# Rebuilding the tail of a fused two-layer kernel: gated cell in 128-token chunks, batches overlapped, and the experts' second layer in row tiles

## What is computed

```python
x = x + xattn(_layernorm(x), ctx)      # 16 heads of 32, softmax, Wq Wk Wv Wo
x = x + experts(_layernorm(x))         # 32 experts x 4 sets: argmax over groups of 32 tokens
x = x + gated(_layernorm(x), ctx)      # 8 heads of 64, q = norm(x), k = v = ctx
x = x + bitlinear(gelu(bitlinear(_layernorm(x), W1, b1)), W2, b2)   # 512 -> 2048 -> 512
```

```python
cs = cumsum(log_sigmoid(fg))                         # forget gates
log_D[i, j] = cs[i] - cs[j] + ig[j]   for j <= i     # else -inf
D = exp(log_D - max_j log_D)
C = (q @ k.T / 8) * D
h = C / (max(|sum_j C|, exp(-max log_D)) + 1e-6) @ v
h = h * rsqrt(mean(h * h) + 1e-6)
```

## Time and profile before

| | us |
|---|---|
| median of 3 runs | 2611.24 (2610.79 to 2611.46) |
| the profiled execution, its own time | 2620.14 |
| its span, first to last instruction | 2618.4 |
| attention, experts, tail in that span | 0 to 1107, 1113 to 1478, 1485 to 2618 |
| mean granted clock of the tensor engine, share of full | 0.902 |

### The profile page before, as it was taken

How to read it: one execution, slowest core, us unless ns; L and a number is a source line. 1 busy time by engine, 2 the same in 40 slices (tenths; PEclk the granted TensorE clock), 3 DMA queues, 4 the chain that set the end, 5 groups by cost and what they waited for, 6 DMA issues and landing times. The chain is left out here.

```text
span 2618.4 us, 43758 instructions
## 1 busy us (share of the span) xinstructions
PE 2216.2 (85%) x14571; PEld 1398.9 (53%) x14571; DVE 1524.9 (58%) x2958; ACT 1347.6 (51%) x2952; POOL 616.1 (24%) x1020
## 2 busy tenths in 40 slices
PE   7999999999999999678788449696979797979755
PEld 3666666666666666375484127353535353535432
DVE  2767676767676767423323225766666666666664
ACT  3666565656565655223324237564646454555543
POOL 1332323131323132031120012313131313131310
PEclk9999999999999999889999767797979797979777
DMA  6334343434343333166756764222122222222100
GB/s 189 95 102 137 82 137 84 138 81 139 78 142 81 109 79 103 49 176 175 239 158 201 257 237 170 97 69 81 68 81 68 81 68 81 68 81 68 37 13 17
DMA packets 193553, 289.05 MB, mean 110 GB/s; under 512 B 29440, under 2 KB 93984, under 8 KB 188128
## 3 DMA queue, kind: packets, MB, share of 16 engines
q1 hardware_dynamic: 134384, 200.32, 24.2%
q10 hardware_dynamic: 42608, 52.97, 6.4%
q0 software_dynamic: 16384, 33.59, 5.0%
HBM read 156.62 MB, written 63.05 MB: 84 GB/s over the span
## 5 line engine op out<-in xcount | busy, mean ns | idle before, releaser
L499 DVE TENSOR_REDUCE a_negmax<-a_score 128x1 f32<-128x512 f32 x512 | 346.5, 685 | 117.2 <-PE a_score L614 109.0
L434 ACT ACTIVATE a_prob<-a_score,a_negmax 128x512 f32<-128x512 f32 x512 | 354.2, 694 | 94.4 <-DVE a_negmax L499 93.5
L316 POOL DMA_DIRECT2D a_q_stack<-a_q_parts x512 | 250.8, 498 | 513.1 <-DVE a_q_parts L493 253.8
L614 PE MATMUL a_score<-a_k_stack,a_q_stack 128*128 128x512 f32 x512 | 354.6, 693 | 9.5 <-ACT a_prob L434 7.6
L622 PEld LDWEIGHTS a_turn<-a_ident,a_prob 128*128 128x128 f32 x2048 | 254.2, 141 | 134.6 <-issue 93.2
L622 PE MATMUL a_turn<-a_ident,a_prob 128*128 128x128 f32 x2048 | 309.3, 274 | 3.4 <-ACT a_perm L410 2.0
L324 DVE COPY a_probT<-a_turn 128x512 f32<-128x512 f32 x256 | 176.4, 689 | 215.8 <-PE a_turn L622 215.6
L324 ACT COPY a_probT<-a_turn 128x512 f32<-128x512 f32 x256 | 150.2, 587 | 285.3 <-PE a_turn L622 283.7
L1253 POOL TENSOR_SCALAR c_diag<-c_negm,c_aL 128x128 f32<-128x128 f32 x256 | 165.5, 664 | 362.2 <-DVEq L1474 127.5
L1711 PE MATMUL c_work<-c_xT,c_cT 64*128 64x512 f32 (+3 forms) x512 | 185.2, 510 | 39.7 <-DVE c_decay L1480 39.7
L1711 PEld LDWEIGHTS c_work<-c_xT,c_cT 64*128 64x128 f32 x512 | 105.2, 215 | 138.7 <-issue 74.4
(11 more groups left out here) (196 smaller groups left out, 3732.8 us busy)
## 6 DMA issues: line engine op xcount, KB each, us to landing
a_k_stack<-a_k_parts SPq DMA_DIRECT2D x512, 64.0 KB, 2.7
a_q_stack<-a_q_parts POOLq DMA_DIRECT2D x512, 64.0 KB, 2.3
scratch_res<-b_res SPq DMA_DIRECT2D x32, 1024.0 KB, 4.6
c_res<-scratch_res SPq DMA_DIRECT2D x32, 1024.0 KB, 9.6
b_xn<-scratch_xn SPq DMA_DIRECT2D x68, 256.0 KB, 2.7
c_hid<-in_L_ffn_W ACTq DMA_DIRECT2D x16, 1024.0 KB, 5.1
c_negm<-scratch_m SPq DMA_DIRECT2D x64, 256.0 KB, 3.4
a_xs<-in_x ACTq DMA_DIRECT2D x8, 1024.0 KB, 5.3
```

Source lines behind the costliest of these rows:

```text
L316: eng.dma_start(stack[kind][i * DH0:(i + 1) * DH0, M % 2, g, :].bitcast(F32), parts[kind][g * DH0:(g + 1) * DH0, part, :].bitcast(F32)).th ...
L434: nc.scalar.activation(prob[:, U % 4, :], score.bank(U)[:, :], ACT.Exp, bias=negmax[:, u:u + 1], accum_out=sums[:, head_of(U), tile_of(U): ...
L499: nc.vector.tensor_reduce(negmax[:, U % UNITS:U % UNITS + 1], score.bank(U)[:, :], AX.X, ALU.max, negate=True).then_inc(max_ready, 1)
L614: nc.tensor.matmul(score.bank(U)[:, :], stack["Q"][:, M % 2, g, t * P:(t + 1) * P], stack["K"][:, M % 2, g, :], start=True, stop=True).the ...
```

## The change

**Attention.** SP stores `cT` of each batch, 1 MB, to a new scratch tensor, between key stacks 2 and 3; ACT waits for that store before it writes the next batch's `cT`. The two query-stack semaphores are made in `build` and cleared at the end.

**Experts.** `inner` loses its zeros: one relu of 128 partitions per expert (4 per group instead of 16), and the second layer multiplies the 32 partitions of a set by 32 rows of `w2T`. The waits for the four result banks come first, the four matmuls follow together.

```diff
-        inner = sb("inner", [P, 2, NE, SETS, G])
+        inner = sb("inner", [P, 2, NE, G])
...
-                nc.gpsimd.memset(inner[:, :, :, :, :], 0.0).then_inc(zeroed, 1)
...
                                 for s in range(SETS):
                                     work.wait_free(pe, h * WORK + GATHERED, 4 * e + s)
-                                    nc.tensor.matmul(work.bank(s)[:, :], inner[:, (j - 1) % 2, e % NE, s, :], w2T[:, e % 2, :],
+                                for s in range(SETS):
+                                    r = slice(s * F, (s + 1) * F)
+                                    nc.tensor.matmul(work.bank(s)[:, :], inner[r, (j - 1) % 2, e % NE, :], w2T[r, e % 2, :],
                                                      start=True, stop=True).then_inc(work.full[s], 1)
...
-                                for s in range(SETS):
-                                    r = slice(s * F, (s + 1) * F)
-                                    last = nc.scalar.activation(inner[r, j % 2, e, s, :], aux.bank(j)[r, e * G:(e + 1) * G], ACT.Relu,
-                                                                bias=b1c[r, bass.ds(h * XH + (j * NE + e), 1)])
+                                last = nc.scalar.activation(inner[:, j % 2, e, :], aux.bank(j)[:, e * G:(e + 1) * G], ACT.Relu,
+                                                            bias=b1c[:, bass.ds(h * XH + (j * NE + e), 1)])
```

```diff
+    PERIOD = (("XQ", 0, -1), ("SCO", 0, 0), ("UP", 0, -1), ("W", 0, 0), ("ST", 0, 0), ("SC", 0, 1),
+              ("SCO", 1, 0), ("W", 1, 0), ("MIX", 0, 0), ("UP", 1, -1), ("W", 2, 0), ("ST", 1, 0), ("SC", 1, 1),
+              ("SCO", 2, 0), ("W", 3, 0), ("MIX", 1, 0), ("HT", 0, -1), ("DN", 0, -1), ("ST", 2, 0), ("SC", 2, 1),
+              ("SCO", 3, 0), ("W", 4, 0), ("MIX", 2, 0), ("SC", 3, 1), ("UP", 2, -1), ("W", 5, 0), ("ST", 3, 0),
+              ("HT", 1, -1), ("DN", 1, -1), ("MIX", 3, 0), ("XT", 0, 1), ("W", 6, 0), ("UP", 3, -1), ("G", 0, 1), ("W", 7, 0),
+              ("HT", 2, -1), ("DN", 2, -1), ("ROWS", 0, 1), ("HT", 3, -1), ("DN", 3, -1))
...
+                    for n in range(3):
+                        chain.step(nc.gpsimd.tensor_tensor(sq, dst, dst, ALU.mult))
+                        chain.step(nc.gpsimd.tensor_tensor(sq, sq, val, ALU.mult))
+                        chain.step(nc.gpsimd.tensor_scalar(sq, sq, -0.5, 1.5, ALU.mult, ALU.add))
+                        chain.step(nc.gpsimd.tensor_tensor(dst, dst, sq, ALU.mult))
...
+                        act.wait_ge(masked, i + 1)
+                        if i >= 4:
+                            wait_full(act, "MIX", (i - 4) // H1, (i - 4) % H1 // 2, h % 2)
+                        nc.scalar.activation(decay[:, h % 4, :], negm[:, h % 4, :], ACT.Exp).then_inc(decay_ready, 1)
...
+                    step(nc.vector.tensor_copy(st[:, 0, :], bank[:, 0:DV]))
+                    for c in range(1, LATER):
+                        last = nc.vector.scalar_tensor_tensor(st[:, c, :], st[:, c - 1, :], gbc[:, p % 2, c * P - 1:c * P],
+                                                              bank[:, c * DV:(c + 1) * DV], ALU.mult, ALU.add)
...
+                    for t in range(T):
+                        for k in range(2):
+                            last = nc.tensor.matmul(work.bank(j + k)[:, cols(t)], cT[half(k), p, cols(t)], xT[half(k), p, cols(t)],
+                                                    start=True, stop=True)
...
+                        for i in range(T):
+                            last = nc.tensor.matmul(mix.bank(j + k)[:, i * DV:(i + 1) * DV], decay[:, (2 * p + k) % 4, cols(i)],
+                                                    head_of(v, 2 * p + k)[:, i], start=i == 0, stop=i == 0, skip_group_check=True)
...
+                    for i in range(1, T):
+                        for k in range(2):
+                            last = nc.tensor.matmul(mix.bank(j + k)[:, i * DV:(i + 1) * DV], xg[half(k), p % 2, cols(i - 1)],
+                                                    state[half(k), p % 2, i - 1, :], start=False, stop=True, skip_group_check=True)
```

The last third of a period on DVE (own is batch m, old is f = m - 1, new is n = m + 1):

```diff
+                    if new:
+                        shifts(0, n)
+                    if own:
+                        states(m, 3)
+                    if old:
+                        scale_hidden(f, 2)
+                        finish(f, 1)
+                    if not old:
+                        clip_weight(6)
+                    if own:
+                        norms(m)
+                    if old:
+                        expand(f, 3)
+                        quantize_hidden(f, 2)
+                    if not old:
+                        clip_weight(7)
+                    if own:
+                        scale_heads(m)
+                    if new:
+                        rows(n)
+                    if old:
+                        scale_hidden(f, 3)
+                        finish(f, 2)
+                    if own:
+                        stats_x3(m)
+                    if new:
+                        columns(n)
+                    if own:
+                        shifts(1, m)
+                    if old:
+                        quantize_hidden(f, 3)
+                    if own:
+                        token_scales(m)
+                        quantize_tokens(m)
+                    if old:
+                        finish(f, 3)
```

1217 lines of the change are left out of this document (714 added, 503 removed).

## The result

The changed kernel takes 2648.9 us (median of 4 runs, 2648.3 to 2655.1) against 2611.4 for the kernel before in the same session: 1.0147 times as long, with 1.013 to 1.0165 as the 95% interval. The forecast was 2503. It is slower where faster was expected.

What follows compares the result with a forecast made beforehand. PE was taken to bound attention, latency of serial chains the tail. Span 2618.4 - 25 (experts) + 3 (first scores) - 61 (middle periods) - 12 (first) - 14 (last with a cell) + 1 = 2510, so 2503 us as median; range 2380 to 2605.

Steps and rivals of the forecast that it cites:

- rival 3: Tail: DVE and POOL hold each other up, +14 and +8 us, periods of 140, total 2655, slower; chance 0.11.
- The middle periods: Tail: walking DVE's order gives 118 us per period instead of 128.2, ends 104 and 130; six save 61.
- The clock: Middle period: `down` after a pause takes 5.3 us instead of 3.6, three or four bursts; +5 us per period.
- POOL's small steps: Middle period: 12 Newton steps in a chain on POOL, taken at 0.3 us each, between 0.1 and 0.6.
- First period: Tail's first period: ACT works some 62 us, then the same chain to `xq`; 92 instead of 104.5, saving 12 (0 to 25).
- Experts: Second-layer stages: fewer relus put three groups of four on the path, saving 12.5 us per stage, 25 in all.
- Until the first scores: Tail's start: one more MB at 4.4 us, fewer transposes and copies about 2 less; +3 us (0 to +10).
- Last with a cell: Tail's last period with a cell: front and scatter are missing; 100 instead of 113.6, saving 14 (0 to 30).
- Last feed-forward: End of the tail: same order, so 0, and +1 us for the second clearing of semaphores.
- row tiles: Experts' second layer: 32-row matmuls taken at the same time as 128-row ones, no gain, since PE is not waited for.
- DVE as the bound: Rival for the tail: overlap works and DVE's work bounds it, periods of 88 us, total 2290; chance 0.10.
- Experts that stay: Rival for the experts: their stages keep their length, paced by transfers, total 2528; chance 0.12.

Runs made afterwards that it cites:

- e7: e5 with POOL starting the heads' four additions only after DVE has scaled all four tiles; 2555.9 us, 0.9757 of the kernel before.
- e11: e9 with states, scatter and mix moved ahead of `down` on PE, and gelu 2 and `down` 1's copies ahead of normalizations on ACT; 2454.1 us, period 106.0.
- e12: e11 with the next batch's fourth scatter moved ahead of `down` 0 and the mix of pair 2 on PE; 2420.1 us, period 99.8.
- e10: e9 with 16, 32, 22 and 6 extra matmuls ahead of the four `down`, covering PE's waits; 2531.5 us, period 115.1.
- e9: Changed kernel with e2's and e4's orders, POOL's b2 additions behind next masks and keys, batch 0's `cT` and `v` loaded behind late `res`; 2535.5 us, period 117.6.
- e3: Changed kernel with 12 extra constant matmuls ahead of every `down`; 2636.4 us, 1.0081 of the kernel before, period 127.8.
- e4: Changed kernel with another order in the first period alone, weight pieces behind each pair's mix on PE; 2627.8 us, first period 111.8 instead of 135.4.
- e8: Kernel before with only the experts' change, second-layer matmuls reading all 128 rows instead of 32, results wrong; 2604.6 us in one run.
- e5: Changed kernel with e2's and e4's orders, batch 1's loads behind batch 0's gate rows, POOL's b2 additions behind next masks and keys; 2556.2 us, period 117.7.
- e2: Changed kernel with ACT's copies for `down` 2 ahead of the chunk weights and those for `down` 3 ahead of the tokens' rounding; 2624.7 us, period 126.1.

## Why the prediction was wrong

**The sign.** It came out on the slow side, close to rival 3's 2655, but by luck and not by rival 3's mechanism. That rival rested on one addition of the kernel before, the longest of eight:

```profile
L1532 DVE TENSOR_TENSOR c_gate_rows<-c_gate_rows x8: 678/679/1475, 1548.0 to 2435.0; 8x512 f32<-8x512 f32 x8
```

It priced DVE's lengthening at 14 us a period and POOL's at 8. In the changed kernel, what each operation of the six middle periods took beyond the shortest of its line and operands adds up to 2.8 us a period on DVE, 2.0 of them the scalings, and 4.7 on POOL. Two steps on 4 columns (L1745 and L1747, 0.97 and 1.31 us) are long in every period, while their like (L1775, L1776) take 0.15 and 0.20; an estimate from these puts 2 us more on DVE. And e7 took the contention away at its largest place and the period did not move. A number that fits is no proof of its cause.

**The middle periods, 118 forecast, 129.5 measured.** The walk on DVE named nearly all the right waits and gave them too little. From `finish` 3 on, end of each step in the period from 2088.8 us, in us:

| step | forecast | after | more than forecast since the row above |
|---|---|---|---|
| expand 0 | 9 | 7.3 | -1.7 |
| largest value 1 | 27 | 25.9 | +0.6 |
| states 2 | 32 | 34.6 | +3.7 |
| expand 2 | 44 | 49.5 | +2.9 |
| largest value 2 | 52 | 59.1 | +1.6 |
| finish 1 | 56 | 64.3 | +1.2 |
| norms | 63 | 72.5 | +1.2 |
| scaling | 71 | 83.6 | +3.1 |
| rows | 80 | 95.6 | +3.0 |
| finish 2 | 86 | 104.4 | +2.8 |
| xq written | 104 | 123.8 | +1.4 |
| finish 3 | 109 | 129.5 | +0.7 |

Of the 20.5 us, 9 had been priced (handovers 4, clock 5). The other 11.5, six times, are the 69 us of the miss. They are not one cause but many small ones, eleven of twelve rows of one sign, which is the failed step: in a walk every wait is the difference of two estimates, and I took the later engine as if it came promptly each time. The wait for states 2 was put at 4.6 and was 7.8; for the gates' logs 3 and was 4.9; for `finish` 2 3 and was 5.1; the scatter's 3.8 was left out; the scalings were taken at their undisturbed length. The engine that came late was mostly ACT, whose work was put at "near 50" us and was 58.4. One part of that can be read: the 32 small squares of a period before and their 32 reads of the sum add up to 13.8 us in durations, but they overlap and kept ACT busy for 8.5, so replacing them (2.4 now) gave back 6 us and not 11. Taken one at a time, each of these misses is small. Most of them are a matter of order, as the experiments show: e11 and e12 took 18 us from a period with the same work. That the period was just inside the prediction's end of 130 while the total lay outside its range is due to the other stretches, three of which came out beyond their own bounds or had none.

**The clock.** Priced at +5 per period, "three or four bursts". In e10, on the order of e9, covering the waits gave 2.5 net; in the changed kernel's own order only e3's part of it was measured, 1.7. As far as these show, the term was too high rather than too low; what all four downs lose in the changed kernel's own order was not measured. The long `up` 2 was no such burst (e3's timeline), and a shorter `down` can only help where DVE waits for it.

**POOL's small steps** were put at 0.3 us each in a chain; they took 0.28 with their gap (12 steps from 2197.1 us, 3.4 us). Right.

**First period, -12 forecast, +31 measured.** The step that failed is "the same chain to `xq`" with "ACT works some 62 us": I summed work and did not walk the first period at all. ACT's work was 57, even less than said. The loop across three engines, with two weight buffers, cost 24 of the 43 us of the miss (e4). The other 19 stay open: the mean clock was 0.60 in the changed kernel, 0.67 in e4 and 0.74 before, and no run takes its part from the rest.

**Experts, -25 forecast, -14 measured.** The place was right, the size not: I gave the path three groups of four in both stages, 12.5 us each (three times 4.3 is 12.9). From the first to the last second-layer matmul it was 91.6 and 90.5 us before and is 87.0 and 84.9 after, 10.2 us together, so little more than one group's 4.3 per stage was on the path. The row tiles at 0 were right (e8). The memset at 0 was right within 1 us: DVE's first instruction stands 6.7 us after PE's instead of 9.4, but the first second-layer matmul comes 95.3 us after attention's end instead of 96.1. About 3 us more came between the two stages (89.4 to 86.2 us), which I had left alone; no run tests that by itself.

**Until the first scores, +3 forecast (0 to +10), +11.5 measured.** The added megabyte was costed at its bytes, 4.4 us. What counted was where it and `v` stood in SP's queue: 5.9 us of the 11.5 is that (e9), and the rest is open. My first explanation after the result, that 4.8 MB more ahead of the scores make the difference, was wrong too: e5 moved 3.25 MB away and nothing came.

**Last with a cell, -14 forecast, -17.5 measured.** Inside its bounds of 0 to 30; it was not walked either, so the closeness proves little. **Last feed-forward, +1 forecast, +9.5 measured.** I called its order the same; it was not, XQ had come behind the late `down` 3 (e2 gives back 7.3).

**Rivals.** DVE as the bound (88) is where e12 heads: 99.8 with 71.6 us of work; no run reached 88. Experts that stay did not happen, more than half the gain came. The chances were too steep: 0.87 for faster rested on a walk whose middle case was a near-best case, while the period from which the change loses, some 134 in my own sum, lay only 16 us above it. It lost already at 129.5, because the first period and the stretches at both ends lost too.

## What to carry to other kernels

When a rebuilt stage is priced by walking its order, walk every stretch that has an order of its own, the first and the last included, and add to each wait what the measured waits of the old kernel show rather than the smallest that the order allows. Where the order of the statements sets the time, removing work need not shorten it (230 us less on PE, 37 us slower); look on each engine for the item that waits longest and ask what stands behind it without needing it: four rounds of such exchanges (e2, e5, e11, e12) were worth 30 us per period here. Before long transfers are added to a queue, look at what is issued behind them, and not only at their bytes.
